# First layer of a two-layer model: recurrence halves alternate on TensorE, heads are gathered before one output matmul, mixing weights use 32 rows, some elementwise steps move to GpSimd, and the order of every step comes from tables

## The reference, cut to what matters

```python
xn = _layernorm(x, axis=-1)
x = x + _L0_attn_ref(xn, ...) + _L0_ffn_ref(xn, ...)
xn = _layernorm(x, axis=-1)
x = x + _L1_attn_ref(xn, ...) + _L1_ffn_ref(xn, ...)
```

```python
xp = jnp.tanh((x + delta * mu0) @ W_x0.T)          # 5 groups of 32
mus = jnp.einsum('blnr,hnr->blnh', xp, W_x2.reshape(HID, 5, R)) + x_bias
r = (x + delta * mu_r) @ W_r.T                     # w, k, v, g alike
...
o_t = einsum('bhk,bhkv->bhv', r_t, S + u * kv); S = exp(w_t) * S + kv
```

```python
w = softmax(t @ expert_emb); topw, topi = top_k(w, 2)
hmid = gelu(einsum('td,edi->tei', t, W1) + b1)     # exact gelu
eo = einsum('tei,eio->teo', hmid, W2) + b2
comb = (sel * topw[:, :, None]).sum(axis=1)
return comb.reshape(bs, L_, d) @ Wo + bo
```

## Time and profile before

| | us |
|---|---|
| median of 3 runs (lowest to highest) | 1784.9 (1777.38 to 1789.67) |
| the profiled execution's own time | 1785.12 |
| its span, first to last instruction | 1783.8 |
| first layer with its streams, 40 to 701 us: span | 661 |
| busy in it: PE / DVE / ACT / POOL | 581.9 / 456.5 / 401.5 / 111.4 |
| second layer, 701 to 1784 us: span | 1083 |
| busy in it: PE / DVE / ACT / POOL | 883.5 / 715.9 / 480.3 / 249.4 |

### The profile page before, as it was taken

How to read it: one execution, slowest core, us unless ns; L and a number is a source line. 1 busy time by engine, 2 the same in 40 slices (tenths; PEclk the granted TensorE clock), 3 DMA queues, 4 the chain that set the end, 5 groups by cost and what they waited for, 6 DMA issues and landing times.

```text
span 1783.8 us, 27062 instructions
## 1 busy us (share of the span) xinstructions
PE 1486.4 (83%) x10080; PEld 668.4 (37%) x10080; DVE 1194.5 (67%) x2874; ACT 894.1 (50%) x1183; POOL 383.1 (21%) x355
## 2 busy tenths in 40 slices
PE   4797998989898997565878988888887988888886
PEld 1233333323332332332433444454444544444432
DVE  5777579467847855887565667766677666776623
ACT  2566656575656665312434544534545354444453
POOL 5021202111211122043320003304242051420024
PEclk7899989799888998556888999979999898999998
DMA  7222212122212211313343223324343142442212
GB/s 244 77 96 73 90 61 92 58 74 73 89 54 68 93 68 43 75 31 88 107 125 90 85 80 109 101 62 117 96 114 96 52 136 86 118 114 76 82 54 55
DMA packets 136834, 156.14 MB, mean 88 GB/s; under 512 B 15712, under 2 KB 99168, under 8 KB 136320
## 3 DMA queue, kind: packets, MB, share of 16 engines
q1 hardware_dynamic: 116560, 131.39, 24.4%
q0 software_dynamic: 8192, 16.79, 3.3%
q10 hardware_dynamic: 11952, 6.23, 1.3%
HBM read 109.80 MB, written 44.56 MB: 87 GB/s over the span
## 4 chain that ended last, share of the span: by engine, by line
PE 34%; DVE 13%; issue 4%; ACT 3%; DMA 1%; another core or an unknown queue 1%; SPq 1%; POOL 0%; ACTq 0%; DVEq 0%; POOLq 0%
PE sh_bank L2245 6%; PE ax_sums L1755 6%; PE sh_bank L2281 5%; DVE wide L1699 4%; PE sh_bank L2256 4%; PE wide L1668 4%; PE wide L1777 3%; DVE am_top L1704 3%; ACT ax_prob L1809 2%; DVE m_hid L2345 1%; PE wide L1785 1%; DMA m_rows<-slot_tokens 1%; PE sh_bank L2268 1%; PE sh_bank L1972 1%; PE wide L1782 1%
## 5 line engine op out<-in xcount | busy, mean ns | idle before, releaser
L1809 ACT ACTIVATE ax_prob<-wide 128x1024 f32<-128x1024 f32 (+1 forms) x320 | 298.4, 939 | 299.0 <-PE wide L1785 109.6
L493 ACT ACTIVATE m_act_h<-m_up,const 128x1024 f32<-128x1024 f32 x256 | 280.5, 1112 | 207.9 <-PE m_up L453 207.1
L1699 DVE CUSTOM_DVE_ANT_0 wide<-wide,const 128x384 f32<-128x384 f32 (+3 forms) x512 | 238.5, 518 | 104.4 <-PE wide L1668 95.1
L2181 POOL DMA_INDIRECT x<-slot_results,mr_slots x128 | 121.9, 952 | 480.5 <-PE wide L1785 173.1
L1668 PE MATMUL wide<-al_ks,al_qs 48*128 48x512 bf16 (+3 forms) x768 | 127.6, 358 | 110.3 <-DVE am_top L1704 41.2
L1704 DVE TENSOR_REDUCE am_top<-wide 128x2 f32<-128x1024 f32 x128 | 156.3, 1223 | 92.7 <-PE wide L1668 87.5
L539 POOL TENSOR_TENSOR m_prod<-m_prod 128x512 f32<-128x512 f32 x64 | 89.8, 1404 | 526.8 <-DVE m_prod L509 526.7
L2165 POOL DMA_INDIRECT slot_tokens<-mr_zn,mr_slots x128 | 123.9, 968 | 338.7 <-PE wide L1668 207.2
L1755 PE MATMUL ax_sums<-ax_prob,al_vs 128*32 128x512 f32 (+3 forms) x1536 | 173.6, 525 | 9.0 <-ACT ax_prob L1809 9.0
L453 PE MATMUL m_up<-m_terms,w1s 96*128 96x512 bf16 x512 | 156.3, 401 | 12.4 <-ACT m_act_h L493 12.4
L470 PE MATMUL m_sums<-m_act_h,const 128*32 128x512 f32 x1024 | 147.4, 650 | 10.7 <-ACT m_act_h L493 6.1
(11 more groups left out here) (298 smaller groups left out, 2154.8 us busy)
## 6 DMA issues: line engine op xcount, KB each, us to landing
m_wt<-in_experts SPq DMA_DIRECT2D x92, 384.0 KB
m_share<-shares SPq DMA_DIRECT2D x128, 256.0 KB
m_rows<-slot_tokens SPq DMA_DIRECT2D x92, 128.0 KB
slot_results<-m_y SPq DMA_DIRECT2D x92, 128.0 KB
stack<-mp_part SPq DMA_DIRECT2D x48, 128.0 KB
m_terms<-stack SPq DMA_DIRECT2D x64, 96.0 KB, 2.0
qstack<-ap_qpart SPq DMA_DIRECT2D x48, 128.0 KB
al_qs<-qstack SPq DMA_DIRECT2D x32, 192.0 KB, 3.5
```

The lines of the kernel that those rows point to most:

```text
L493: A.activation(self.act_h[:, slot, :, :], self.up[u][:, :, :], ACT.Gelu, bias=self.w("b1", 4 * half + ep, 4 * half + ep + 1)).then_inc(sel ...
L1699: p = V.tensor_tensor_reduce(tile[:, x, first:first + n], tile[:, x, first:first + n], self.w("later_s", TILE - n, TILE), -1.0, 3e38, ALU. ...
L1809: A.activation(dst, src, ACT.Exp, scale=SCALE).then_inc(*wide.empties("sum", i, u))
```

## The change

Nothing of what is computed changes. In the first layer:

- the two halves' matmuls alternate in the block products, the chunk sums and the outputs, with one carrier for both;
- the mixing weights use 32 rows each, half 0 and half 1 on different rows (the table `wx2` and the tanh results exist on both row groups);
- four head products go by four 32-column matmuls into one bank that puts the heads side by side (`tensor_fold`, 16 times); two of these banks are added on VectorE, and one matmul with the plain `Wo` follows for each tile (`tensor_out` of `Moe0`, 8 times);
- the token additions of the five mixtures (40 instructions) and four router steps (32 instructions) move from VectorE to GpSimd;
- places come from tables of numbers, one for each engine; share buffers go from 4 to 3.

In the second layer the mask matmuls are cut into four of 64 rows, and two small constants are cast more.

```diff
-TOP2_STEPS = 17
+TOP2_STEPS = 13
+PREP = {"h": (-10.255, -9.943), "hi": (-10.025, -9.891), "logits": (-9.659, -9.423), ...
...
+TENSOR_AT = {"low0": 0.428, "low1": 0.925, "mus1": 1.292, "hid": 1.633, "mus2": 1.704, "key": 2.447, ...
...
 def tensor_mus(self, it, i):
-            E.matmul(self.bank(f"mus{i}_{s}", it)[:, :], self.w(f"wx2{i}"), self.low[s][i // 4][:, :], ...
+        for s in range(2):
+            first = 32 * ((i % 4) ^ s)
+            rows = slice(first, first + 32)
+            E.matmul(self.bank(f"mus{i}_{s}", it)[:, :], self.w(f"wx2{i}")[rows, :], self.low[s][i // 4][rows, :], ...
...
 def tensor_blocks(self, it, use, keys, recs, width):
         for s in range(2):
-            b = self.bank(...)
-            e.wait_ge(*self.free(...))
-            self.carrier(b)
-            for j in range(NJ):
+            e.wait_ge(*self.free(names[s], it))
+        self.carrier(self.bank(names[0], it))
+        for j in range(NJ):
+            for s in range(2):
...
 def tensor_fold(self, p):
-        for j in range(2):
-            e.wait_ge(self.folded, 2 * p + j + 1)
-            last = E.matmul(self.sums[m][:, :], self.w("wo0", hd * HID, (hd + 1) * HID), self.prod[2 + j][:, :], start=j == 0, stop=j == 1)
+        e.wait_ge(self.folded, 4 * p + 4)
+        for q in range(4):
+            last = E.matmul(self.sums[m][32 * q:32 * q + 32, :], self.w("gather", 32 * (p % 2), 32 * (p % 2) + 32), self.both[q][:, :], start=True, stop=True)
+def tensor_out(self, i):
+        e.wait_ge(*self.sums.done(SUM_NUMBER["fold", 2 * i + 1]))
+        E.matmul(self.sums[m][:, :], self.w("wo0"), self.comb[:, :], start=True, stop=True).then_inc(self.sums.filled, 1)
...
+def gpsimd_mixtures(self):
+                for s in range(2):
+                    g.wait_ge(*self.done(f"mus{i}_{s}", it))
+                    G.tensor_tensor(m[:, :], m[:, :], self.tokens(it, s), ALU.add).then_inc(self.mix_made, 1)
...
+def gpsimd_weights(self):
+            G.tensor_tensor(logits, logits, wide(self.peak), ALU.subtract)
+            G.tensor_tensor(one, one, eq, ALU.add)
+            G.tensor_tensor(one, one, logits, ALU.mult)
+            G.tensor_tensor(one, one, wide(self.sum), ALU.mult)
...
+def forbid(self, tile, x, keys, both, off):
+        rows, n = slice(half * x, half * x + half), half * (keys + 1)
+        place = self.k.bf["ident" if keys == x else "swap"][rows, :]
```

More of the change, by code:

```diff
@@ L231, in tensor @@
             e.wait_ge(*up.free(n))
[L232 removed]
+            e.wait_ge(self.weighted, 4 * i + 4)
             for m in range(NC):
@@ L416, in __init__ @@
         self.act_h = sb("act_h", [P, self.ACT_SLOTS, 2, TILE])
-        self.prod = [sb(f"prod{n}", [P, TILE]) for n in range(4)]
+        self.prod = [sb(f"prod{n}", [P, TILE]) for n in range(2)]
+        self.both = [sb(f"both{n}", [P, TILE]) for n in range(4)]
+        self.comb = sb("comb", [P, TILE])
         self.terms_landed = [k.sem(f"m0_terms_landed{n}") for n in range(self.TERM_SLOTS)]
@@ L526, in gn_added, with out_in_front @@
         return (f"go{s}", it) if self.rw.gn_slot(it, "add") < place else None
-    def folds_in_front(self, t, place):
-        folds = [SUM_NUMBER["fold", p] for p in range(FOLDS) if UNITS[2 * p][0] == t and fold_place(p) < place]
-        return max(folds) if folds else None
+    def out_in_front(self, t, place):
+        i = ORDER.index(t)
+        return SUM_NUMBER["out", i] if out_place(i) < place else None
     def gpsimd(self):
         G, g = self.k.nc.gpsimd, self.k.pool
-        for p in range(FOLDS):
+        for p in range(PAIRS_OF_UNITS):
             for j in range(2):
@@ L565 @@
-for _h in LEVELS:
-    PLACES += [f"factors{_h}", f"scale{_h}", f"scale{_h}b", f"place{_h}", f"lev{_h}"]
-PLACES += ["placelast", "fill", "qk", "kct", "add", "state", "out", "copy"]
-WIDTHS = [1.5 if n <= PLACES.index("selves") else 0.8 if n < PLACES.index("placelast") else 7.0 if place == "out" else 1.0 for n, place in enumerate(PLACES)]
-TENSOR_LAG = {"low1": 0.2, "rate": 0.6, "self": 1.2, "kct": 0.5, "add": 0.7} | {f"lev{h}": 1.5 for h in LEVELS}
-SCALAR_LAG = {place: 0.5 for place in PLACES} | {"rate": 1.2, "place64": 0.0, "lev64": 2.0, "fill": 1.0, "kct": 1.0}
@@ L573 @@
-VECTOR_LAG = {"low0": -1.0, "low1": -0.4, "rate": 2.4, "selves": 1.0, "add": 1.4, "state": 0.5} | {f"mus{i}": 0.5 for i in range(5)}
-def turn_at(it, x):
-    n = max(int(x), 0)
-    return RW_START + 16 * (it + (sum(WIDTHS[:n]) + (x - n) * WIDTHS[n]) / sum(WIDTHS))
-def out_piece(s, n):
-    return PLACES.index("out") + 0.2 + 0.1 * (NC * s + n)
+USES += ["lev64_00", "lev64_10", "lev64_01", "lev64_11", "kct", "add", "out0", "out1"]
+TENSOR_AT = {"low0": 0.428, "low1": 0.925, "mus1": 1.292, "hid": 1.633, "mus2": 1.704, "key": 2.447, "rate": 2.901, "mus0": 3.102, "rec": 3.452, "mus3": 3.98, "val": 4.734, "mus4": 5.252, "gate": 5.681, "self": 6.718, "lev1": 7.83, "lev2": 8.114, "lev4": 8.867, "lev8": 9.717, "lev16": 10.309, "lev32": 11.154, "lev64": 12.104, "lev64b": 12.352, "kct": 12.704, "add": 13.359, "out0": 13.855, "out1": 14.03, "out2": 14.066, "out3": 14.986}
@@ L680, in mix_slot, with at @@
         return 10 * it + 2 * MIX_ORDER.index(i) + s
-    def at(self, it, place, lags):
-        return self.slot(it, PLACES.index(place) + lags.get(place, 0.0))
+    def at(self, it, place, table):
+        return turn_at(it, table[place])
     def halves(self, t, h):
@@ L792, in tensor @@
                             e.wait_ge(*self.free(f"lev64_{s}{half}", it))
-                            self.carrier(b)
-                            for n2 in range(2):
-                                cc = 2 * half + n2
-                                p = E.matmul(b[0:64, n2 * 256:n2 * 256 + 256],
+                        self.carrier(self.bank(f"lev64_0{half}", it))
+                        for n2 in range(2):
+                            cc = 2 * half + n2
+                            for s in range(2):
+                                p = E.matmul(self.bank(f"lev64_{s}{half}", it)[0:64, n2 * 256:n2 * 256 + 256],
@@ L892, in scalar @@
                         p.then_inc(*self.empties(f"lev32_{s}", it))
-                    yield self.at(it, "lev64", SCALAR_LAG)
-                    for s in range(2):
-                        yield self.at(it, "lev64", SCALAR_LAG) + s * 0.8 * 16 / sum(WIDTHS) * 0.8
-                        for half in range(2):
+                    for half in range(2):
+                        yield self.at(it, "lev64b" if half else "lev64", SCALAR_AT)
+                        for s in range(2):
                             use = f"lev64_{s}{half}"
@@ L1757, in weigh @@
         p.then_inc(self.weighed, 1)
+    def forbid(self, tile, x, keys, both, off):
+        half = CH // 2
+        rows, n = slice(half * x, half * x + half), half * (keys + 1)
+        place = self.k.bf["ident" if keys == x else "swap"][rows, :]
+        later = self.k.bf["earlier_t" if keys == x else "earlier_s"][rows, 0:n]
+        if both:
+            dst, later = tile[:, x, :].rearrange("p (a n) -> p a n", a=2)[:, :, 0:n], later.unsqueeze(1).broadcast_to([half, 2, n])
+        else:
+            dst = tile[:, x, off:off + n]
+        return self.k.nc.tensor.matmul(dst, place, later, start=False, stop=True, skip_group_check=True)
     def tensor(self):
@@ L1779, in tensor @@
                 if blk >= 4 * th:
-                    for x in range(2):
-                        if len(pairs) > 1:
-                            p = E.matmul(tile[:, x, :].rearrange("p (a n) -> p a n", a=2)[:, :, 0:CH], self.k.bf["ident"],
-                                         self.k.bf["earlier_t"].unsqueeze(1).broadcast_to([P, 2, CH]), start=False, stop=True, skip_group_check=True)
-                        else:
-                            p = E.matmul(tile[:, x, off:off + CH], self.k.bf["ident"], self.k.bf["earlier_t"], start=False, stop=True, skip_group_check=True)
+                    for keys in range(2):
+                        for x in range(2):
+                            p = self.forbid(tile, x, keys, len(pairs) > 1, off)
                 p.then_inc(wide.filled, 1)
```

371 lines of the change are left out of this document (204 added, 167 removed).

## The result

| | before | changed |
|---|---|---|
| median of four (lowest to highest) | 1781.14 us (1774.34 to 1789.67) | 1694.8 us (1691.49 to 1697.66) |
| ratio, 95% interval | | 0.9494 (0.9459 to 0.9529) |
| profiled execution, its span | 1785.12, 1783.8 us | 1697.66, 1696.3 us |
| first layer ends at | 701 us | 608 us |
| second layer | 1083 us | 1088 us |

A forecast was written before the change was run, and what follows sets the result against it. TensorE was taken to bound the first layer: 99 us of its work removed, less 15 us of new idle time, gives 84 us; with 7 us from the second layer, 91 us off 1785.1 gives 1694 us, range 1650 to 1748 us.

The forecast's parts named there:

- idle time grows by 15 us: First layer, 70 to 690 us: TensorE's idle time taken as 80 us in place of 64.5.
- first rival: First layer: engines wait for each other instead, TensorE's idle time doubles to 128 us; 1745 us, chance 0.13.
- gathered heads: First layer: 64 full matmuls become 16 groups of four narrow ones and 8 full ones; 39.8 us saved.
- alternation with its carriers: First layer: alternating halves saves 25.3 us on wide levels and outputs, 9 on L710; halving the carriers saves 6.3.
- mixing weights: First layer: 40 full matmuls become 20 pairs on different rows, 44.2 to 25.2 us; 19.0 us saved.
- Overlap of row halves: TensorE: matmuls on different row groups run at the same time; two on 32 rows take 0.57 of two full ones.
- second rival: TensorE: the halves don't overlap, so only gathered heads and carriers pay; 1754 us, chance 0.06.
- L710's rate: Low levels and tokens' own products, 35.5 us: alternating saves 17.8 if the array limits, nothing if record rate does; 9 taken.
- VectorE's stretch: First layer: added GpSimd work lengthens VectorE's steps by 0 to 72 us; 18 us taken, as most read PSUM.
- mixture path: First layer: later token additions cost 1.3 us for each of 20 pairs, 26 us uncovered; a third counted.
- slower rival through GpSimd's queue: First layer: mixture additions queue on GpSimd and stop projections, 6 us for each of 20 pairs; 1799 us, chance 0.05.
- masks: Second layer: splitting the mask matmuls by row halves takes 16 us off TensorE and 7 us off the time.

The follow-up runs named there:

- groups 1 and 3: Two sets of follow-up runs, each on one chip, with the changed kernel rerun unchanged: 1667.79 us, ratio 0.9417, and 1666.48 us, ratio 0.9437.
- o_back: Changed kernel with the old places and with mixtures and router steps back on VectorE, TensorE's savings kept: 1757.27 us, ratio 0.9861.
- u_order: Changed kernel with every first-layer place computed by the old list of steps, all other parts kept: 1749.78 us, ratio 0.988.
- u_work: Changed kernel with all of TensorE's first-layer work put back, tables and GpSimd steps kept: 1744.77 us, ratio 0.9787.
- again: Changed kernel run once more as it is, against the kernel before: 1667.79 us, ratio 0.9417.
- again2: Changed kernel run unchanged once more, as base on another chip, against the kernel before: 1666.48 us, ratio 0.9437.
- u_place: Changed kernel with three TensorE steps placed later and two ScalarE numbers following, no work changed: 1663.72 us, ratio 0.9424.

## Why the number was right, and which step was not

**The number came out of a wrong split, and its closeness is luck.** The forecast's gain was 84 us in the first layer and 7 in the second; in the first pair of profiles it is 93 (701 to 608) and -5 (1083 to 1088). In groups 1 and 3 the changed kernel took 102 and 100 us less than the kernel before, where the forecast said 91. The prediction had TensorE's work count one for one, 99 us less 15 us of new idle time, and counted the tables at nothing. Measured, the tables (with the GpSimd steps) bring 34 to 43 us and the savings bring about 50 on top of them (658 to 604 to 608). Together they are the 93 us that stand beside the forecast 84.

**The step that failed is "idle time grows by 15 us", taken whatever the order.** With the old places it grows by 42 to 48 us, to 121 (o_back) and 127 us (u_order), and u_order's 1749.78 us is near the first rival's 1745. It is not that rival's mechanism: from 70 to 690 us the idle time goes from 64.5 to 620 - 509.0 = 111 us, not to 128, and it is waits for VectorE's placing and for the rate that grow (28.2 us for 11.3, 15.8 for 4.4), while TensorE's wait for the gelu is 11.6 us, less than before. With the tables the idle time does not grow at all. The order comparison before the run showed the moved rows, but their worth was never put in the sum as a term.

**The sum had no term for the clock.** It took durations "at this trace's mean clock", 0.92. Under the old places the clock falls to 0.87 and 0.88 when the work is removed, and busy time falls by 59 to 67 us in place of 92. Work and busy time are not the same: putting all the work back under the tables (u_work) raises busy time by 68 us, at a clock of 0.95, and fills 15 us of idle time, so the layer ends 53 us later than in again. The single terms, as the end of the first layer saw them: gathered heads 33 to 36 of a forecast 40; alternation with its carriers 26 to 30 of 25 + 9 + 6 = 40; mixing weights 0 of 19. They add up to 59 to 66 us, more than the 50 to 53 us that undoing all three costs, so they are not independent of each other.

**What held.** *Overlap of row halves*, against the second rival: L822, L808 and L857 fell to 45% of the former. *L710's rate*: 22.8 us, between the 18 of the array and the 35 of the record rate. The rate is not a fixed one, since 13 ns a record is possible when they alternate, and it did not halve either. The Trainium skill's figure of about 25 ns between starts ("TensorE: Matmul & The Clock Gate", Part 1, on the warm-up mystery) is one for matmuls, and a float32 matmul leaves two records. The prediction set 20 ns a record against it, which compares two different things. An estimate by matmuls, with the mean length of one record (225 ns in the earlier trace rows, 237 ns above) taken off the run: (650 - 225) / 15 = 28 ns between starts before, which the figure allows, and (860 - 237) / 31 = 20 ns where halves alternate, which lies under it. *GpSimd*: 191.5 us for about 196. *VectorE's stretch*: some 25 us for 18, though its ground was wrong: not most VectorE steps read PSUM but, by the trace of before, 272 of 726 from 70 to 690 us. *First layer's end*: 608 for 617.

**Terms of the wrong size.** The *mixture path*: a third of 26 us more wait for the late additions was counted. TensorE waits for them 2.1 + 2.0 + 1.1 = 5.2 us in all, before L756 and L872 as in again2's rows above, and before L790:

```profile
L790 PE MATMUL rw_bank<-rw_mix,const 128*128 128x512 f32 x16 | 8.7, 630 | 2.0 <-POOL rw_mix L1111 2.0
```

(of the changed kernel's first profile, where the other two waits are the same). So the slower rival through GpSimd's queue, which wanted 5.3 us a pair, is not there. The *masks*: 9 to 24 us of TensorE and 10 to 15 us of time, where 16 and 7 were counted. One group of records of the changed kernel shows it, where the former pair took 37.9 + 25.5 us; the stretch's row holds L1807 alone:

```profile
608.00:1696.00 1088.00, 56.17 (x768) 38.64 (x768) 0.88 0.31 89
```

By this row, under 60 us as forecast, only 7 us are gone; the rest of the 9 to 24 us would be overlap with the scores ahead and the product behind, and the clock, which these runs don't separate.

**What stays open.** How the tables' 34 to 43 us divide among TensorE's, VectorE's and ScalarE's numbers was not tried, nor the tables without the GpSimd steps under TensorE's old work, nor four share buffers in place of three. Nor was a version that takes the 128-row mixing weights in the first turn alone, where the clock is higher with them, and the narrow ones after it. u_place, at 1663.72 us the fastest median of its group, can't be told from the changed kernel.

## What to carry to other kernels

Work taken off the fullest engine counts only as far as the order lets its queue close up: when a change brings new places with it, price the places as a term of their own, by the waits that stop the fullest engine while other work stands ready behind them. Allow for the clock taking a part back: an engine with less to do in a stretch that already has gaps may be granted less, and then all its other work there takes longer. And a wait that stays when its step is moved points to a producer that is late, not to a step in the wrong place.
